# Five edits to a fused two-layer FFN kernel: adapter copies, a wait moved, a group on another engine, a last tile in two parts

## The chip, the cores and the metric

The kernel runs on one core of one Trainium2 chip. The metric is the device time of one execution in microseconds (us). Engines are TensorE (PE in the rows), VectorE (DVE), ScalarE (ACT), GpSimd (POOL) and SyncE (SP), which issues most transfers; its queue is SPq. Each engine runs its own instructions in order, and semaphores order the engines among themselves.

## The reference

Two layers act on `x`, 1024 tokens by 512 features. Each is `x = x + ffn(cond(x))`.

```python
# layer 0: gated net with low-rank adapters picked by token block, then a gated FFN with scaled weights
gate = x @ Wg.T + lora(x);  up = x @ Wu.T + lora(x)        # 1376 hidden
c = (silu(gate) * up) @ Wd.T + lora(...)
f = anemll(silu(anemll(c, gate)) * anemll(c, up), down)     # w_eff = w * (su @ sv), 1792 hidden
x = x + f
# layer 1: one adapted linear, then a gated FFN with group-scaled int4 weights
c = x @ W.T + b + 2 * (x @ A[id]) @ B[id]
f = (silu(c @ Wg.T) * (c @ Wu.T)) @ Wd.T                    # W[o, i] = q[o, i] * s[o, i // 128]
x = x + f
```

## The kernel before, in words

Tokens lie along the free axis in two chunks of 512, features along the partitions in tiles of 128. A float32 operand is split into a rounded part (`_hi`) and a rest (`_lo`), and a product is the sum of three (`hi*hi`, `hi*lo`, `lo*hi`), except with int4 weights, which need two. ScalarE writes the `_hi` parts (activation with Copy), VectorE the `_lo` parts (`lo`, L1221). A written-out order per engine and semaphores decide everything: there is no scheduler.

The phases run in order: `cond` gate/up and down, `ffn0` gate/up and down in two halves, `cond1`, and then the int4 FFN in groups.

**`ffn0` gate/up** takes each weight tile's 2x2 blocks in Strassen's way: seven block products per tile instead of eight (`seven_tile`), issued for tile 0 in the order 2, 6, 4, 3, 1, 5, 7 and for later tiles 2, 3, 1, 4, 5, 6, 7. VectorE scales the raw weights (L1238, L1228), forms their block sums (`block_sums`, L1458, L1461, L1463), subtracts the rests (`piece_lo`), and adds up the products (`part_sum`, `diff`, `gate`, `up`). For tile 0 the product 6 is in `ps_down[0]`, and `seven_gate1` (L1495) reads it; product 3 of tile 1 writes this bank. Behind product 1 of tile 1 TensorE makes scales for the next pair of tiles (`pair_scales`, L1797), which waits for two scale products of VectorE.

**`ffn0 down b`** has four output tiles. Between its second and third, and third and fourth, the adapter rows of `cond1` are made (`hi_of_b1`, `lo_of_b1`), two of four pairs each time. The rows stand in `b1_rows` in four quarters of 32 partitions: hi, lo, hi, lo. `down_adapters` reads them in `cond1`.

**The int4 FFN** runs in two halves (`part`), each of 7 gate/up tiles ("units") and then 4 `down` tiles. A group is one 128-column block of int4 weights times 1024 tokens, four matmuls into one of four PSUM banks in turn. Each group must be read out with its scale, by ScalarE (`scaled`, the first and third) or by VectorE with an add (`added`, L1346), before its bank is used again four groups later (`bank_free`). GpSimd adds partial sums (`unit_join` L809), multiplies half of the tokens of silu(gate) and up (`unit_product` L815), makes `act_lo` (`unit_lo` L820) and adds the `down` results into `xp` (`down_sums` L826, L830, L833). VectorE multiplies the other half (`unit_product` L1354). The `down` groups (o, k) go: (0,0..4), (1,0..4), (0,5), (1,5), (0,6), (1,6), (2,0..6), (3,0..6).

The last `down` tile of the second half uses int4 groups for the first 512 tokens (`half_group`), added up by VectorE (L1406 is the last step), and weights scaled beforehand for the other 512 (`last_rest`, 21 matmuls, added by L1410 in two pieces). SP sends the outputs in order, L720 and L722.

Of the kernel before, what the change touches and what calls it, by code (L numbers as in the profile page):

```python
# [138 lines left out]
def plan_groups():  # L139
# [8 lines left out]
    for part in range(2):  # L148
# [14 lines left out]
def adaln_ffn(nc, d, out):  # L163
# [7 lines left out]
    with ExitStack() as ctx:  # L171
# [79 lines left out]
        down_more = [place(f"down_more{n}", [P, TOK], F32, x) for n, x in enumerate((at["lora_b1"], at["lora_b1"] + 4 * KB, at["h"] + 28 * KB))]  # L251
        w_int = place("w_int", [P, 2, WT], I32, at["w"] + 16 * KB)
# [57 lines left out]
        b1_hi_done, b1_step, b1_ready = sem("b1_hi_done"), sem("b1_step"), sem("b1_ready")  # L310
# [26 lines left out]
        rest_ready, last_sum = sem("rest_ready"), sem("last_sum")  # L337
        sum_done = sem("sum_done")
# [91 lines left out]

        def int_slot(n):

            return (named["cond1"].s0 + HK - 2 + n) % 2
# [163 lines left out]
        def _(sp):  # L597
# [54 lines left out]
            for ph in phases:  # L652
# [74 lines left out]
        def _(pool):  # L727
# [120 lines left out]
        def _(act):  # L848
# [50 lines left out]
            def hi_of_b1(pair):  # L899
# [4 lines left out]
                nc.scalar.activation(b1_rows[quarter(0), pair, :], raw, ACT.Copy)  # L904
                nc.scalar.activation(b1_rows[quarter(2), pair, :], raw, ACT.Copy).then_inc(b1_hi_done, 1)
# [46 lines left out]
            def unit_hi(u):  # L952
                for c in range(CH):
                    act.wait_ge(half_done[c], u + 1)
# [6 lines left out]
            def group_tile(n, u, begun):  # L961
# [3 lines left out]
                if u > 2:  # L965
                    for c in range(CH):
                        act.wait_ge(half_done[c], u - 2)
# [10 lines left out]
            def group_down(n, part, o):  # L978
# [7 lines left out]
                if o == 0:  # L986
                    unit_silu(last)
                if n + 2 < 2 * (ACT_TILES + HK):
# [222 lines left out]
        def _(dve):  # L1211
# [137 lines left out]
            def unit_product(u):  # L1349
# [3 lines left out]
                gate = gate_sum[:, u % 4, chunk(0)]  # L1353
# [815 lines left out]
```

## Time and profile before

| | |
|---|---|
| median of 3 runs | 640.85 us (640.57 to 641.29) |
| the profiled execution: time, span | 641.1 us, 639.5 us |
| TensorE busy | 627.1 us, 98% of the span |
| VectorE, ScalarE, GpSimd busy | 464.0, 322.0, 245.0 us |
| a matmul of 128x512 | about 0.39 us shown, one issued every 0.23 us |

Busy times overlap. In a timeline row a start and a duration stand first, and in brackets how long the engine was idle before it and who released it. A duration can hold a wait inside the instruction. A merged row (x2, x4) covers several instructions.

### The profile page before, as it was taken

Reading aid. Unit: us, or ns where it says so; the run is one execution under the profiler, and the core shown is the slowest. Engines: PE = TensorE matmul, PEld = TensorE weight load, DVE = VectorE, ACT = ScalarE, POOL = GpSimd, SP = SyncE. Lnnn points to the kernel's source line nnn. Section 1 sums busy time; section 2 is a strip of 40 time slices with the busy share of each in tenths; the row PEclk is TensorE's granted clock in tenths of the full one; section 3 lists DMA queues with packets and bytes.
Section 4 is the critical chain, followed back from the end, with each engine's and each line's share of the span. In section 5 each row is a group of like instructions: output and inputs, shape, how many; then the busy total and the mean of one; then the engine's idle time right before and its main releaser. Section 6 shows DMA issues by size and latency. Waiting matters only on the chain.

```text
span 639.5 us, 7875 instructions
## 1 busy us (share of the span) xinstructions
PE 627.1 (98%) x2843; PEld 514.0 (80%) x2843; DVE 464.0 (73%) x569; ACT 322.0 (50%) x430; POOL 245.0 (38%) x192
## 2 busy tenths in 40 slices
PE   8999999999999989999999999999999999999997
PEld 6888888888878878788888778887887887788875
DVE  5576674534467997885447888647688999999997
ACT  5674725244535344442113453435557886578850
POOL 3550020000000025752023666430003888959986
PEclk9999999999999999999999999999999999999999
DMA  8750132101021112311102011240223111221203
GB/s 251 167 149 20 33 92 79 66 1 45 19 73 43 57 34 68 130 58 58 39 27 99 33 34 45 71 86 16 69 92 99 61 58 63 99 67 61 87 0 133
DMA packets 24186, 44.51 MB, mean 70 GB/s; under 512 B 9828, under 2 KB 11876, under 8 KB 24100
## 3 DMA queue, kind: packets, MB, share of 16 engines
q1 hardware_dynamic: 22100, 40.80, 20.8%
q0 software_dynamic: 2048, 3.22, 1.9%
q8 instruction: 23, 0.38, 0.2%
q14 instruction: 15, 0.12, 0.1%
HBM read 40.59 MB, written 2.10 MB: 67 GB/s over the span
## 4 chain that ended last, share of the span: by engine, by line
PE 79%; DVE 8%; ACT 5%; issue 4%; POOL 2%; DMA 1%; SPq 0%; DVEq 0%; ACTq 0%
PE ps_down L1747 7%; PE ps_down L1749 7%; PE ps_down L1748 7%; PE ps_up L1747 3%; PE ps_up L1748 3%; PE ps_up L1749 3%; PE ps_m L1918 3%; PE ps_gate L1918 3%; PE ps_gate L1919 3%; PE ps_down L1919 3%; PE ps_m L1919 3%; PE ps_down L1918 3%; PE ps_up L1918 3%; PE ps_up L1919 3%; PE ps_gate L1747 2%
## 5 line engine op out<-in xcount | busy, mean ns | idle before, releaser
L782 POOL TENSOR_TENSOR act_lo<-up,act_hi 128x512 fp32r<-128x512 f32 x14 | 18.2, 1300 | 194.6 <-ACT act_hi L1033 194.6
L1747 PE MATMUL ps_down<-act_hi,w_hi 128*128 128x512 f32 (+1 forms) x180 | 70.7, 393 | 1.0 <-DVE xp L1568 1.0
L1749 PE MATMUL ps_down<-act_hi,w_lo 128*128 128x512 f32 (+1 forms) x180 | 70.2, 390 | 0.0
L1748 PE MATMUL ps_down<-act_lo,w_hi 128*128 128x512 f32 (+1 forms) x180 | 70.2, 390 | 0.0
L809 POOL TENSOR_TENSOR up_sum<-up_sum,up_more 128x1024 f32<-128x1024 f32 x14 | 33.8, 2413 | 67.0 <-DVE up_more L1346 67.0
L1221 DVE TENSOR_TENSOR w_lo<-w_raw,w_hi 128x512 fp32r<-128x512 f32 (+4 forms) x41 | 44.7, 1090 | 16.0 <-ACT w_hi L866 10.4
L866 ACT ACTIVATE w_hi<-w_raw 128x1024 fp32r<-128x1024 f32 (+4 forms) x30 | 27.0, 900 | 46.0 <-DVE w_raw L1228 23.1
L1221 DVE TENSOR_TENSOR b_rows<-b_raw,b_hi 32x1024 fp32r<-32x1024 f32 (+2 forms) x27 | 28.1, 1042 | 19.9 <-ACT b_rows L884 12.0
L1747 PEld LDWEIGHTS ps_down<-act_hi,w_hi 128*128 128x128 f32 (+1 forms) x180 | 33.8, 188 | 8.1 <-DVE w_lo L1221 1.4
L1749 PEld LDWEIGHTS ps_down<-act_hi,w_lo 128*128 128x128 f32 (+1 forms) x180 | 33.8, 188 | 7.2
L1748 PEld LDWEIGHTS ps_down<-act_lo,w_hi 128*128 128x128 f32 (+1 forms) x180 | 33.8, 188 | 6.8
L820 POOL TENSOR_TENSOR act_lo<-gate_sum,act_hi 128x1024 fp32r<-128x1024 f32 x14 | 39.2, 2806 | 0.0
L944 ACT ACTIVATE act_hi<-gated 128x512 fp32r<-128x512 f32 (+1 forms) x22 | 13.8, 632 | 49.8 <-DVE gated L1330 49.8
L1346 DVE SCALAR_TENSOR_TENSOR gate_sum<-ps_up,s_group,gate_sum 128x1024 f32<-128x1024 f32 x28 | 35.8, 1279 | 3.9 <-PE ps_up L1919 3.9
L1747 PE MATMUL ps_up<-h_hi,w_hi 128*128 128x512 f32 (+1 forms) x96 | 37.7, 393 | 0.3 <-DVE w_lo L1221 0.3
L1748 PE MATMUL ps_up<-h_lo,w_hi 128*128 128x512 f32 (+1 forms) x96 | 37.6, 392 | 0.0
L1749 PE MATMUL ps_up<-h_hi,w_lo 128*128 128x512 f32 (+1 forms) x96 | 37.4, 390 | 0.0
L1027 ACT ACTIVATE w_hi<-w_total 128x512 fp32r<-128x512 f32 (+1 forms) x28 | 20.7, 739 | 32.6 <-POOL w_total L776 21.5
L1568 DVE TENSOR_TENSOR xp<-xp,ps_down 128x512 f32<-128x512 f32 x20 | 13.5, 683 | 28.7 <-PE ps_down L1749 27.3
L1221 DVE TENSOR_TENSOR w_lo<-w_total,w_hi 128x512 fp32r<-128x512 f32 (+1 forms) x28 | 25.4, 909 | 10.8 <-ACT w_hi L1027 10.5
L1747 PE MATMUL ps_gate<-h_hi,w_hi 128*128 128x512 f32 (+1 forms) x80 | 31.6, 395 | 0.5 <-DVE h_lo L1221 0.3
L1861 PE MATMUL ps_gate<-x_hi,w_hi 128*128 128x512 f32 x80 | 31.5, 394 | 0.0
(292 smaller groups left out, 1858.4 us busy)
## 6 DMA issues: line engine op xcount, KB each, us to landing
w_int<-in_ffn_gu SPq DMA_DIRECT2D x14, 512.0 KB, 3.5
w_raw<-in_cond_gu SPq DMA_DIRECT2D x9, 512.0 KB, 4.3
w_raw<-in_ffn_gu SPq DMA_DIRECT2D x9, 512.0 KB, 3.5
w_raw<-in_ffn_dn SPq DMA_DIRECT2D x8, 448.0 KB, 3.2
w_int<-in_ffn_dn SPq DMA_DIRECT2D x8, 448.0 KB, 3.2
xp<-in_x SPq DMA_DIRECT2D x8, 256.0 KB, 5.1
w_raw_third<-in_ffn_gu SPq DMA_DIRECT2D x4, 512.0 KB, 3.4
xp<-in_x SPq DMA_DIRECT2D x1, 2048.0 KB, 10.7
```

The lines of the kernel that those rows point to most:

```text
L809: nc.gpsimd.tensor_tensor(up_sum[:, u % 3, :], up_sum[:, u % 3, :], up_more[:, u % 2, :], ALU.add).then_inc(up_done, 1)
L820: nc.gpsimd.tensor_tensor(act_lo[:, j, :], gate_sum[:, u % 4, :], act_hi[:, j, :].bitcast(F32), ALU.subtract).then_inc(unit_ready, 1)
L866: nc.scalar.activation(w_hi[:, s, n], w_raw[:, s, n], ACT.Copy).then_inc(w_hi_done, 1)
L1027: nc.scalar.activation(w7_hi[j % 2][:, pieces[piece]], value, ACT.Copy).then_inc(done, 1)
L1221: return nc.vector.tensor_tensor(out_, value, hi.bitcast(F32), ALU.subtract)
L1346: return nc.vector.scalar_tensor_tensor(out=here, in0=group_bank(g), scalar=group_scale(g), in1=here, op0=ALU.mult, op1=ALU.add)
L1747: nc.tensor.matmul(ps[0:m, :], w_hi[0:r, s, cols], rhs_hi(k, r), start=start and n == 0, stop=False)
L1748: nc.tensor.matmul(ps[0:m, :], w_hi[0:r, s, cols], rhs_lo(k, r), start=False, stop=False)
L1749: last = nc.tensor.matmul(ps[0:m, :], w_lo[0:r, s, cols], rhs_hi(k, r), start=False, stop=stop and n == len(ks) - 1)
L1861: nc.tensor.matmul(banks[n][:, :], w7_hi[s][:, cols], x_hi[n][:, k, :], start=not more and k == 0, stop=False, skip_group_check=more)
L1918: nc.tensor.matmul(bank[:, chunk(c)], weights, hi[:, chunk(c)], start=True, stop=False)
L1919: last = nc.tensor.matmul(bank[:, chunk(c)], weights, lo[:, chunk(c)], start=False, stop=True)
```

## The change

1. **Adapter rows of `cond1`.** ScalarE and VectorE write only the first hi and lo quarters; SP copies these 64 partitions to the other 64, two pairs at a time, behind the first and second weight loads of `cond1`.
2. **Tile 1 of the Strassen phase** waits for `gate1_done` at its product 3, no longer at its start. On VectorE, `seven_gate1` of tile 0 stands ahead of two block sums.
3. **Group (1,4)** of each half goes from VectorE to ScalarE, into a buffer `down_extra` of its own, and GpSimd adds it (`extra_sum`). VectorE multiplies all 1024 tokens of a half's last unit, and GpSimd none of them.
4. **`last_rest`** runs as two parts of 256 tokens with 21 matmuls each, in two banks, each followed by its add.

```diff
-                    add(n + o, "d", k, "a" if k in (0, 2) else "v")
+                    add(n + o, "d", k, "a" if k in (0, 2) or (o, k) == (1, 4) else "v")
...
+        down_extra = place("down_extra", [P, TOK], F32, at["gated"])
...
+        def halves_done(u, c):
+            return u + 1 - c * ((u + 1) // ACT_TILES)
...
+        rest_quarters = [(last_bank(n)[:, 0:CT // 2], slice(CT + part * CT // 2, CT + (part + 1) * CT // 2))
+                         for part, n in enumerate((ACT_TILES, 0))]
...
                         load_tile(ph, o // 2, o % 2)
+                        if ph.name == "cond1" and o < 2:
+                            sp.wait_ge(b1_ready, 2 * o + 2)
+                            pairs_of = slice(2 * o, 2 * o + 2)
+                            sp.dma_start(b1_rows[2 * PR:4 * PR, pairs_of, :].bitcast(F32),
+                                         b1_rows[0:2 * PR, pairs_of, :].bitcast(F32)).then_inc(b1_copied[o], 16)
...
+            def extra_sum(part):
+                here = xp[:, 1, :]
+                pool.wait_ge(act_read, group_of[part * (ACT_TILES + HK) + ACT_TILES + 1, "d", 4].ea)
+                nc.gpsimd.tensor_tensor(here, here, down_extra[:, :], ALU.add).then_inc(extra_added, 1)
...
                     unit_join(u)
-                    unit_product(u)
+                    if j + 1 < ACT_TILES:
+                        unit_product(u)
                     if j > 0:
                         unit_lo(u - 1)
                 unit_lo(ACT_TILES * (part + 1) - 1)
+                extra_sum(part)
...
                 nc.scalar.activation(b1_hi[quarter(3), pair, :], raw, ACT.Copy)
-                nc.scalar.activation(b1_rows[quarter(0), pair, :], raw, ACT.Copy)
-                nc.scalar.activation(b1_rows[quarter(2), pair, :], raw, ACT.Copy).then_inc(b1_hi_done, 1)
+                nc.scalar.activation(b1_rows[quarter(0), pair, :], raw, ACT.Copy).then_inc(b1_hi_done, 1)
...
+                if o == 1:
+                    if part:
+                        act.wait_ge(extra_added, part)
+                    scaled(group_of[n, "d", 4], down_extra[:, :])
...
-                lo(b1_rows[quarter(1), pair, :], raw, hi).then_inc(b1_step, 1)
-                dve.wait_ge(b1_step, pair + 1)
-                lo(b1_rows[quarter(3), pair, :], raw, hi).then_inc(b1_ready, 1)
+                lo(b1_rows[quarter(1), pair, :], raw, hi).then_inc(b1_ready, 1)
...
-                gate = gate_sum[:, u % 4, chunk(0)]
-                nc.vector.tensor_tensor(gate, gate, up_sum[:, u % 3, chunk(0)], ALU.mult).then_inc(half_done[0], 1)
+                tokens = chunk(0) if (u + 1) % ACT_TILES else slice(0, TOK)
+                gate = gate_sum[:, u % 4, tokens]
+                nc.vector.tensor_tensor(gate, gate, up_sum[:, u % 3, tokens], ALU.mult).then_inc(half_done[0], 1)
...
+                if (q, n) == (1, 3):
+                    pe.wait_ge(gate1_done, 1)
...
-                if q == 1:
-                    pe.wait_ge(gate1_done, 1)
...
                 pe.wait_ge(last_ready, 2)
+                for n, (bank, tokens) in enumerate(rest_quarters):
+                    if n == 1:
+                        pe.wait_ge(act_read, groups[-ACT_TILES].ea)
```

What stands where on an engine, first VectorE in the Strassen phase, at the end of tile 0. `part_sum`, `gate` and `up` are tile 0's partial results, `w_total` the block sums and `w_lo` the rests of tile 1's weights, and `ps_*` the banks. Before:

```order
L1221 TENSOR_TENSOR w_lo_91<-w_total_95,w_hi_89 128x512 [waits piece_hi_done]
L1461 TENSOR_TENSOR w_total_95<-w_raw 128x256
L1463 TENSOR_TENSOR w_total_95<-w_raw 128x512
L1495 TENSOR_TENSOR gate_0_106<-ps_down,part_sum_100 128x512 [waits part_done,seven_done]
L1538 TENSOR_TENSOR part_sum_100<-part_sum_100,ps_gate 128x512 [waits seven_done,part_done]
L1221 TENSOR_TENSOR w_lo_91<-w_total_95,w_hi_89 128x768 [waits w_hi_done]
L1550 TENSOR_TENSOR up_0_102<-ps_gate,part_sum_100 128x512 [waits seven_done,rest_done]
```

After the change:

```order
L1250 TENSOR_TENSOR w_lo_91<-w_total_95,w_hi_89 128x512 [waits piece_hi_done]
L1524 TENSOR_TENSOR gate_0_106<-ps_down,part_sum_100 128x512 [waits part_done,seven_done]
L1490 TENSOR_TENSOR w_total_95<-w_raw 128x256
L1492 TENSOR_TENSOR w_total_95<-w_raw 128x512
L1567 TENSOR_TENSOR part_sum_100<-part_sum_100,ps_gate 128x512 [waits seven_done,part_done]
L1250 TENSOR_TENSOR w_lo_91<-w_total_95,w_hi_89 128x768 [waits w_hi_done]
L1579 TENSOR_TENSOR up_0_102<-ps_gate,part_sum_100 128x512 [waits seven_done,rest_done]
```

The `gate` sum (L1495 before, L1524 now) moved ahead of both block sums.

GpSimd at the end of the second half, from the last unit on, `act_lo` being the rests and `xp` the output. Before:

```order
L809 TENSOR_TENSOR up_sum<-up_sum,up_more 128x1024 [waits dve_read]
L815 TENSOR_TENSOR gate_sum<-gate_sum,up_sum 128x512 [waits up_done,gate_done]
L820 TENSOR_TENSOR act_lo<-gate_sum,act_hi 128x1024 [waits unit_hi_done] x2
L826 TENSOR_TENSOR xp<-xp,down_more_123 128x1024 [waits dve_read]
L830 TENSOR_TENSOR xp<-xp,down_sum 128x1024 [waits dve_read,more_added]
L826 TENSOR_TENSOR xp<-xp,down_more_124 128x1024 [waits dve_read]
L830 TENSOR_TENSOR xp<-xp,down_sum 128x1024 [waits dve_read,more_added]
L826 TENSOR_TENSOR xp<-xp,down_more_122 128x1024 [waits dve_read]
L833 TENSOR_TENSOR xp<-xp,down_sum 128x512 [waits dve_read,more_added]
```

After the change:

```order
L826 TENSOR_TENSOR up_sum<-up_sum,up_more 128x1024 [waits dve_read]
L837 TENSOR_TENSOR act_lo<-gate_sum,act_hi 128x1024 [waits unit_hi_done] x2
L842 TENSOR_TENSOR xp<-xp,down_extra 128x1024 [waits act_read]
L850 TENSOR_TENSOR xp<-xp,down_more_123 128x1024 [waits dve_read]
L854 TENSOR_TENSOR xp<-xp,down_sum 128x1024 [waits dve_read,more_added]
L850 TENSOR_TENSOR xp<-xp,down_more_124 128x1024 [waits dve_read,extra_added]
L854 TENSOR_TENSOR xp<-xp,down_sum 128x1024 [waits dve_read,more_added]
L850 TENSOR_TENSOR xp<-xp,down_more_122 128x1024 [waits dve_read]
L857 TENSOR_TENSOR xp<-xp,down_sum 128x512 [waits dve_read,more_added]
```

The 512-column product is gone, so the two `act_lo` follow the join at once, and an add of `down_extra` stands ahead of all other adds.

VectorE at the start of the `down` groups of the second half, from group (0,1) on. Before:

```order
L1346 SCALAR_TENSOR_TENSOR down_sum<-ps_m,s_down,down_sum 128x1024 [waits group_ready,act_read]
L1346 SCALAR_TENSOR_TENSOR down_more_123<-ps_up,s_down,down_more_123 128x1024 [waits group_ready,act_read]
L1354 TENSOR_TENSOR gate_sum<-gate_sum,up_sum 128x512 [waits up_done,gate_done]
L1346 SCALAR_TENSOR_TENSOR down_sum<-ps_gate,s_down,down_sum 128x1024 [waits group_ready,dve_read]
L1346 SCALAR_TENSOR_TENSOR down_sum<-ps_down,s_down,down_sum 128x1024 [waits group_ready,act_read]
L1346 SCALAR_TENSOR_TENSOR down_more_124<-ps_gate,s_down,down_more_124 128x1024 [waits group_ready,act_read]
L1346 SCALAR_TENSOR_TENSOR down_sum<-ps_m,s_down,down_sum 128x1024 [waits group_ready,dve_read]
L1346 SCALAR_TENSOR_TENSOR down_more_123<-ps_down,s_down,down_more_123 128x1024 [waits group_ready,dve_read]
L1346 SCALAR_TENSOR_TENSOR down_more_124<-ps_up,s_down,down_more_124 128x1024 [waits group_ready,dve_read]
```

After the change:

```order
L1373 SCALAR_TENSOR_TENSOR down_sum<-ps_m,s_down,down_sum 128x1024 [waits group_ready,act_read]
L1373 SCALAR_TENSOR_TENSOR down_more_123<-ps_up,s_down,down_more_123 128x1024 [waits group_ready,act_read]
L1382 TENSOR_TENSOR gate_sum<-gate_sum,up_sum 128x1024 [waits up_done,gate_done]
L1373 SCALAR_TENSOR_TENSOR down_sum<-ps_gate,s_down,down_sum 128x1024 [waits group_ready,dve_read]
L1373 SCALAR_TENSOR_TENSOR down_sum<-ps_down,s_down,down_sum 128x1024 [waits group_ready,act_read]
L1373 SCALAR_TENSOR_TENSOR down_more_124<-ps_gate,s_down,down_more_124 128x1024 [waits group_ready,act_read]
L1373 SCALAR_TENSOR_TENSOR down_more_123<-ps_down,s_down,down_more_123 128x1024 [waits group_ready,dve_read]
L1373 SCALAR_TENSOR_TENSOR down_more_124<-ps_up,s_down,down_more_124 128x1024 [waits group_ready,dve_read]
```

The product (`gate_sum<-gate_sum,up_sum`) has 1024 columns, and one read of bank `ps_m`, that of group (1,4), is gone.

## Rows read from the trace of the kernel before

**Rows 1.** Stretches of 20 us: busy time per engine, granted clock, DMA share, GB/s

```profile
...
220.00:240.00 20.00, 18.23 (x83) 14.80 (x82) 19.43 (x32) 9.79 (x17) 4.75 (x4) 1.00 0.17 53
...
620.00:640.00 20.00, 14.94 (x64) 11.51 (x63) 15.33 (x17) 3.30 (x4) 14.03 (x7) 0.94 0.29 106
...
```

**Rows 2.** Waits of TensorE: waiting, waited for, us, times, longest

```profile
...
PE ps_gate L1918 <- DVE down_sum L1346: 1.5, 2, 0.7
...
```

**Rows 3.** Timeline, Strassen tiles 0 and 1 (start, us, idle before and its releaser)

```profile
228.92 0.68 DVE L1221 TENSOR_TENSOR w_lo<-w_total,w_hi 128x512 fp32r<-128x512 f32 x1
...
231.65 0.95 DVE L1221 TENSOR_TENSOR w_lo<-w_total,w_hi 128x768 fp32r<-128x768 f32 x1
...
235.11 0.68 DVE L1238 TENSOR_TENSOR w_raw_third<-w_raw_third,ps_m 128x512 f32<-128x512 f32 x1
...
230.57 0.84 ACT L1027 ACTIVATE w_hi<-w_total 128x768 fp32r<-128x768 f32 x1 [2.11 <-DVE w_total L1463]
...
231.24 0.47 PE L1861 MATMUL ps_up<-x_hi,w_hi 128*128 128x512 f32 x1 [1.49 <-DVE gate L1495]
...
235.85 0.74 PE L1797 MATMUL ps_m<-pack_long,pack_short 128*128 128x256 f32 x4 [0.28 <-DVE w_raw_third L1238]
```

**Rows 4.** Timeline, second and third tile of `ffn0 down b`

```profile
430.29 0.63 ACT L903 ACTIVATE b_hi<-b_raw 32x512 fp32r<-32x512 f32 x1
...
433.51 0.63 ACT L905 ACTIVATE b_rows<-b_raw 32x512 fp32r<-32x512 f32 x1
...
434.17 1.41 DVE L1221 TENSOR_TENSOR b_rows<-b_raw,b_hi 32x512 fp32r<-32x512 f32 x2 [0.53 <-ACT b_rows L905]
435.61 1.09 DVE L1228 TENSOR_TENSOR w_raw<-w_raw,ps_m 128x896 f32<-128x896 f32 x1
...
438.79 1.28 DVE L1568 TENSOR_TENSOR xp<-xp,ps_down 128x512 f32<-128x512 f32 x2
...
438.22 0.39 PE L1749 MATMUL ps_down<-act_hi,w_lo 128*128 128x512 f32 x1
439.61 0.47 PE L1747 MATMUL ps_down<-act_hi,w_hi 128*128 128x512 f32 x1 [1.00 <-DVE xp L1568]
```

**Rows 5.** Timeline, end of the first half; last row groups by line

```profile
530.59 2.42 POOL L809 TENSOR_TENSOR up_sum<-up_sum,up_more 128x1024 f32<-128x1024 f32 x1
533.68 1.30 POOL L815 TENSOR_TENSOR gate_sum<-gate_sum,up_sum 128x512 f32<-128x512 f32 x1 [0.68 <-ACT gate_sum L950]
534.93 2.86 POOL L820 TENSOR_TENSOR act_lo<-gate_sum,act_hi 128x1024 fp32r<-128x1024 f32 x1
...
533.90 1.64 DVE L1354 TENSOR_TENSOR gate_sum<-gate_sum,up_sum 128x512 f32<-128x512 f32 x1
535.46 1.27 DVE L1346 SCALAR_TENSOR_TENSOR down_sum<-ps_gate,s_down,down_sum 128x1024 f32<-128x1024 f32 x1
...
536.78 0.50 PE L1918 MATMUL ps_gate<-act_hi,w_q 128*128 128x512 f32 x1 [0.74 <-DVE down_sum L1346]
...
545.40 0.50 PE L1918 MATMUL ps_m<-act_hi,w_q 128*128 128x512 f32 x1
...
L1354 DVE TENSOR_TENSOR gate_sum<-gate_sum,up_sum 128x512 f32<-128x512 f32 x14 | 11.7, 832 | 0.0
```

**Rows 6.** Timeline, the end of the program

```profile
619.52 2.41 POOL L826 TENSOR_TENSOR xp<-xp,down_more 128x1024 f32<-128x1024 f32 x1 [1.69 <-DVE down_more L1346]
...
631.71 2.55 POOL L833 TENSOR_TENSOR xp<-xp,down_sum 128x512 f32<-128x512 f32 x2
...
621.23 1.12 ACT L959 ACTIVATE down_sum<-ps_down,s_down 128x1024 f32<-128x1024 f32 x1 [0.86 <-PE ps_down L1919]
...
633.35 1.47 DVE L1406 TENSOR_TENSOR xp<-xp,down_sum 128x512 f32<-128x512 f32 x1
...
634.29 0.33 SPq L720 DMA_DIRECT2D out_t<-xp  x1
...
635.81 0.45 SPq L722 DMA_DIRECT2D out_t<-xp  x1
```

More of the change, by code:

```diff
@@ L309, in adaln_ffn @@
         a1_hi_done, a1_ready = sem("a1_hi_done"), sem("a1_ready")
-        b1_hi_done, b1_step, b1_ready = sem("b1_hi_done"), sem("b1_step"), sem("b1_ready")
+        b1_hi_done, b1_ready = sem("b1_hi_done"), sem("b1_ready")
+        b1_copied = [sem(f"b1_copied{n}") for n in range(2)]
         pack_hi_done, pack_step, pack_ready = sem("pack_hi_done"), sem("pack_step"), sem("pack_ready")
@@ L337, in adaln_ffn @@
         rest_ready, last_sum = sem("rest_ready"), sem("last_sum")
+        extra_added = sem("extra_added")
         sum_done = sem("sum_done")
@@ L824, in down_sums @@
                 here = xp[:, o, :]
+                if o == 1:
+                    pool.wait_ge(extra_added, part + 1)
                 pool.wait_ge(dve_read, group_of[n, "d", 5].ev)
@@ L966, in group_tile @@
                     for c in range(CH):
[L967 removed]
+                        act.wait_ge(half_done[c], halves_done(u - 3, c))
                 scaled(group_of[n, "u", 0], up_sum[:, u % 3, :])
@@ L1381, in group_down @@
                     unit_product(ACT_TILES * (part + 1) - 1)
-                dve.wait_ge(dve_read, group_of[n, "d", 1].ev)
-                added(group_of[n, "d", 4], both).then_inc(dve_read, 1)
+                if o != 1:
+                    dve.wait_ge(dve_read, group_of[n, "d", 1].ev)
+                    added(group_of[n, "d", 4], both).then_inc(dve_read, 1)
             def group_down_more(n, part, o):
@@ L1390, in group_down_end @@
             def group_down_end(n, part, o):
-                dve.wait_ge(dve_read, group_of[n, "d", 4].ev)
+                dve.wait_ge(dve_read, group_of[n, "d", 1 if o == 1 else 4].ev)
                 added(group_of[n, "d", 6], down_sum[:, (HK * part + o) % 3, :]).then_inc(dve_read, 1)
             def last_tile(n, m):
-                both, (here, rest) = down_sum[:, m % 3, chunk(0)], (xp[:, HK - 1, chunk(c)] for c in range(CH))
+                both, here = down_sum[:, m % 3, chunk(0)], xp[:, HK - 1, chunk(0)]
                 dve.wait_ge(act_read, group_of[n, "l", 0].ea)
@@ L1406, in last_tile @@
                 nc.vector.tensor_tensor(here, here, both, ALU.add).then_inc(last_sum, 1)
-                dve.wait_ge(rest_ready, 1)
-                bank = last_bank(ACT_TILES)
-                for tokens in (slice(0, CT // 2), slice(CT // 2, CT)):
-                    nc.vector.tensor_tensor(rest[:, tokens], rest[:, tokens], bank[:, tokens], ALU.add).then_inc(last_sum, 1)
+                for n, (bank, tokens) in enumerate(rest_quarters):
+                    dve.wait_ge(rest_ready, n + 1)
+                    rest = xp[:, HK - 1, tokens]
+                    nc.vector.tensor_tensor(rest, rest, bank, ALU.add).then_inc(last_sum, 1)
             def last_weights():
@@ L1928, in last_rest @@
             def last_rest():
-                bank = last_bank(ACT_TILES)
                 pe.wait_ge(last_ready, 2)
-                for k in range(ACT_TILES):
-                    part = int(k * P >= last_cut)
-                    cols = slice(k * P - part * last_cut, (k + 1) * P - part * last_cut)
-                    hi, low = (act[:, k, chunk(1)] for act in (act_hi, act_lo))
-                    nc.tensor.matmul(bank, last_hi[part][:, cols], hi, start=k == 0, stop=False)
-                    nc.tensor.matmul(bank, last_hi[part][:, cols], low, start=False, stop=False)
-                    last = nc.tensor.matmul(bank, last_lo[part][:, cols], hi, start=False, stop=k == ACT_TILES - 1)
-                last.then_inc(rest_ready, 1)
+                for n, (bank, tokens) in enumerate(rest_quarters):
+                    if n == 1:
+                        pe.wait_ge(act_read, groups[-ACT_TILES].ea)
+                    for k in range(ACT_TILES):
+                        part = int(k * P >= last_cut)
+                        cols = slice(k * P - part * last_cut, (k + 1) * P - part * last_cut)
+                        hi, low = (act[:, k, tokens] for act in (act_hi, act_lo))
+                        nc.tensor.matmul(bank, last_hi[part][:, cols], hi, start=k == 0, stop=False)
+                        nc.tensor.matmul(bank, last_hi[part][:, cols], low, start=False, stop=False)
+                        last = nc.tensor.matmul(bank, last_lo[part][:, cols], hi, start=False, stop=k == ACT_TILES - 1)
+                    last.then_inc(rest_ready, 1)
             def bank_free(g):
@@ L1981, in down_adapters @@
                 if ph.name == "cond1":
-                    pe.wait_ge(b1_ready, PAIRS)
+                    for n in range(2):
+                        pe.wait_ge(b1_copied[n], 16)
                     pe.wait_ge(t_hi_rows, 2 * CH + c + 1)
```

5 lines of the change are left out of this document (3 added, 2 removed).

## Prediction

> **What bounds the kernel now.** I read the span in stretches of 20 us first. TensorE is busy nearly everywhere (98% of the span) at the higher of its two clock levels; the two stretches with the most time without it are shown: from 220 us 1.8 us, at a granted clock of 1.00 and with VectorE busy 19.4 of 20, and the last with 5.1 [rows 1]. Then TensorE's waits: 1.5 us go to a VectorE read of a `down` group, twice [rows 2]. So time is won only where TensorE pauses, or behind its last product. Then the timelines of the four places that the diff touches [rows 3 to 6]. All sums are made against the profiled execution's own time, 641.1 us (span 639.5 and 1.6 around it), which is 0.25 above the median, 640.85. No change smaller than about 0.2% (1.3 us) can be told from none.
>
> **Strassen tile 1, expected gain 1.5 us, taken as a loss of 0.4.** TensorE waits 1.49 us before product 2 of tile 1, which starts at 231.24, for the gate sum L1495 [rows 3]. Now only product 3 waits for it, and L1495 stands two instructions earlier. Product 2 can start once the piece subtraction at 228.92 is done, near 229.7, so products 2, 3 and 1 go 1.5 us early. But the next thing in TensorE's queue is a pair of scales that waits for VectorE's second scale product, L1238 at 235.11; before, TensorE already waited 0.28 for it, until 235.85 [rows 3]. VectorE runs with no pause over 0.1 us from 228.92 to there and none of its work goes away, so TensorE only waits later. Worse, the two block sums slip by the 0.60 of L1495. ScalarE's 0.84 us rounding of piece 2 needs them: it started at 230.57 and ended at 231.41, before VectorE wanted it at 231.65. Now it starts at 231.17 and VectorE gets it about 0.88 after its start, at 232.05. VectorE's chain, and with it the scales and all behind, goes from 231.65 to 232.05: **+0.40**. Bounds: 0 if the rounding is quicker than that row, and a gain of 1.5 if VectorE had slack that I can't see.
>
> **Next net's adapter rows.** Each of four pairs loses a ScalarE copy of 0.64 us and a VectorE subtraction with its self wait; in their place stand two transfers. The loss matters for pairs 0 and 1 only: TensorE paused from 438.45 (0.23 after its last issue at 438.22) to 439.61 for the sum L1568 at 438.79 [rows 4]. Before, ScalarE ran six activations from 430.29, the last at 433.51, and VectorE's second pair started at 434.17. With four, ScalarE ends pair 1 at about 432.85, VectorE subtracts from 432.89 to 433.5, and L1228 starts at 433.5, not 435.61: 2.1 us earlier. All up to L1568 hangs on it, so that starts at 436.7 and TensorE does not wait: 439.61 - 438.45 = 1.16, and 0.08 for the first product after a pause, which is slower: **-1.24**. The transfers are issued by SP at about 433.6 and 442; the product that reads the rows runs after 460, and a wait of SP for them ends before the wait of the load behind it (the weight buffer comes free at 437 and 446). So they cost nothing; without that cover each would cost the 2.0 to 2.5 us of an SP transfer. Bounds: gain 1.0 to 1.3.
>
> **End of each half: the product that VectorE takes over.** VectorE's product for unit 6 (L1354) doubles from 512 to 1024 columns; a fourth of a `down` tile's seven groups, (1,4), goes to ScalarE; GpSimd loses its half product and gets a 1024-column add. Before, VectorE asked for L1354 at 533.90, while GpSimd held L815 from 533.68 to about 534.93; the product ended at 535.46, which is 0.53 after GpSimd was done, and GpSimd's next instruction (L820) took 2.86 where a 1024-column one takes 2.4 [rows 5]. So these two instructions ran one after the other. After the change GpSimd has no product at 533.68: it goes from L809 (530.59, done 2.37 later at 532.96) straight into L820, 2.36 long, until 535.32. VectorE asks at 533.90, waits until 535.32, and then needs 1.07 for 1024 columns (twice the 0.53): done at 536.39, **0.93 later** than 535.46. Its next read, L1346, is the one that TensorE waits for: group (1,3) starts at 537.71, not 536.78. After that VectorE has one 1.2 us read less, so the small pause before 545.40 and its slow first products go (0.16 and 0.12 there, 0.12 one group earlier): 0.40 comes back. **+0.53** per half; what is queued behind the product on VectorE are the reads that free banks for TensorE, and ScalarE's rounding of unit 6 behind it, with (1,2) and the new (1,4), is late by 0.9 but ahead of TensorE.
> Without the wait (both engines side by side) the product would end at 533.90 + 1.2 = 535.1, 0.36 earlier than before, and a half would gain 0.76. The mean of all L1354, 0.83 us, seems to speak for this. The Trainium skill (SBUF, State Buffer; section "Who interferes with whom") says that a VectorE instruction with two SBUF inputs and a GpSimd instruction that reads SBUF fully block each other, and whichever comes first keeps the port for its whole length; by it the half loses 0.53, by the mean alone it gains. The rows at 533.90 and 534.93 agree with the rule.
>
> **Behind the second half: GpSimd.** From 619.52 GpSimd adds `down` results without a pause until L833 ends, 631.71 + 2.55, near 634.24 [rows 6]. The new add of `down_extra` comes first. It needs ScalarE's read of (1,4): TensorE's group (1,3) at 614.47 + 0.93 = 615.40, (1,4) 1.05 later at 616.45, ScalarE's read starts 1.10 after the group did and takes 1.12 with 0.04 until others see it, as that of the next `down` tile does at 621.23: 618.71. The add takes 2.36, until 621.07, so the chain starts 1.55 late and ends at 635.79. VectorE's add L1406 now meets it too: it asks near 633.9 while the first L833 runs, gets in between the two, and puts 0.53 on the second: 636.32. SP sends outputs in order, so the send that left at 634.29 leaves at 636.37; the other three follow at the 0.38 at which sends follow each other, and the last leaves at 637.51, not 635.81: **+1.70**, the half's own +0.53 in it.
> The last half tile in two parts is hidden under this: 42 products of 256 columns for 21 of 512. Four with 256 columns and their own weights took 0.74 us with the slow first one [rows 3], against 0.23 of pace for 512, so 42 take 4.8 to 5.1 where 21 took 4.76; VectorE's first part is done before the second is ready and saves 0.33. TensorE's side would end at 636.0, before the sends. Uncovered it is worth -0.2 to +0.1.
>
> **Sum:** +0.40 - 1.24 + 0.53 + 1.70 = +1.39: 642.5 for the profiled execution, **642.2** for the median.
>
> **Rivals.**
> 1. TensorE keeps the 1.5 us of tile 1 (scales not bound by VectorE). Against it: the 0.28 wait at 235.85. Then -1.5 in place of +0.40: sum -0.51, 640.3. Chance 0.12.
> 2. GpSimd is not what ends the kernel, because it catches up or the extra add fits its pause before 619.52 (1.7 us long). Against it: (1,4) is read only by 618.7. Then +0.68 (0.53, 0.15 of shorter products) in place of 1.70: +0.37, 641.2. Chance 0.15.
> 3. The other side: the product is not blocked. Then each half gains 0.76, of which the sends at the end keep 0.15: +0.40 - 1.24 - 0.76 - 0.15 = -1.75, 639.1. It decides from the point where L1354 with 1024 columns ends before 535.2. Against it: the rows at 533.90 and L1406's 1.47 for 512 columns beside L833. Chance 0.09, with mixtures 0.12.
> 4. Worse: the last four sends are closer together than before, so the data queue is what ends; then the shift of the first of them, 2.08, counts whole, and VectorE's delay is not given back (+0.93 for +0.53): 640.85 + 0.40 - 1.24 + 0.93 + 2.48 = 643.4. Chance 0.11.
> The forecast, 641.5 to 642.9, has 0.50.
>
> **Numbers.** 80% range 640.3 to 643.3. Faster by over 0.2% (below 639.6) holds rival 3 and a rest: 0.12. Slower (above 642.1) holds rival 4 and three quarters of the forecast: 0.49. Within: 0.39.
>
> **What would show it.** Right: product 2 of tile 1 near 229.7, and the wait at the scales grown to about 2.5 us; no wait before 439.6 (shifted); the 1024-column product taking over 2.4 us, and TensorE's wait behind it grown to about 1.7; GpSimd's last adds ending after TensorE's last product, and SP waiting for them. Wrong: a product of 1.2 us, or a last send that waits for L1410's successor on VectorE.

## The result and the profile after

In five executions the changed kernel took 644.48 us in the median (643.16 to 644.68), the kernel before 641.29 in the same comparison: a ratio of 1.0044, interval 1.0025 to 1.0062. Slower was right; 644.48 is 2.3 above the 642.2 predicted and 1.2 above the top of the range. Of these 2.3, 0.44 is not the change's: the forecast was counted from 640.85, and the kernel before took 641.29 in this comparison. The change cost 3.2, where 1.4 was forecast.

The profiled execution is the fastest of the five, 643.16, with a span of 641.2 at a mean granted TensorE clock of 0.997. The other four spanned 642.4 to 642.7 at 0.995. So this trace can show where 1.7 us went, and not the rest. First its stretches of 20 us (columns as in [rows 1]) and TensorE's waits, against [rows 1, 2].

```profile
220.00:240.00 20.00, 17.82 (x82) 14.44 (x81) 19.10 (x32) 9.69 (x17) 4.40 (x4) 1.00 0.16 53
620.00:640.00 20.00, 15.34 (x88) 13.28 (x86) 15.04 (x17) 3.83 (x4) 15.73 (x8) 0.94 0.29 106
```

```profile
PE ps_gate L1947 <- DVE down_sum L1373: 3.3, 2, 1.7
PE ps_m L1826 <- DVE w_raw_third L1267: 2.2, 1, 2.2
```

The wait for the gate sum is gone, and the wait for the scale product is 2.2 where it was 0.28; the one for the `down` reads has grown from 1.5 to 3.3. Between 220 and 240 TensorE works less than before, not more. The timeline of tile 1, against [rows 3]:

```profile
229.46 0.68 DVE L1524 TENSOR_TENSOR gate<-ps_down,part_sum 128x512 f32<-128x512 f32 x1
...
231.99 0.96 DVE L1250 TENSOR_TENSOR w_lo<-w_total,w_hi 128x768 fp32r<-128x768 f32 x1 [0.32 <-ACT w_hi L1056]
...
235.46 0.68 DVE L1267 TENSOR_TENSOR w_raw_third<-w_raw_third,ps_m 128x512 f32<-128x512 f32 x1
...
231.11 0.85 ACT L1056 ACTIVATE w_hi<-w_total 128x768 fp32r<-128x768 f32 x1 [2.70 <-DVE w_total L1492]
...
229.06 0.63 PE L1826 MATMUL ps_m<-pack_long,pack_short 128*128 128x256 f32 x4
229.69 0.47 PE L1890 MATMUL ps_up<-x_hi,w_hi 128*128 128x512 f32 x1
...
236.19 0.74 PE L1826 MATMUL ps_m<-pack_long,pack_short 128*128 128x256 f32 x4 [2.18 <-DVE w_raw_third L1267]
```

Product 2 starts 1.55 earlier, the scales 0.34 later (0.40 against the first scales of tile 1, which are at 229.06 here and at 229.12 before). VectorE now waits 0.32 for the rounding on ScalarE. At the adapter rows, against [rows 4], VectorE:

```profile
433.23 0.68 DVE L1250 TENSOR_TENSOR b_rows<-b_raw,b_hi 32x512 fp32r<-32x512 f32 x1 [0.61 <-ACT b_rows L930]
433.94 1.09 DVE L1257 TENSOR_TENSOR w_raw<-w_raw,ps_m 128x896 f32<-128x896 f32 x1
...
437.12 0.68 DVE L1597 TENSOR_TENSOR xp<-xp,ps_down 128x512 f32<-128x512 f32 x1
```

The sum that TensorE needs starts 1.67 earlier, and TensorE has no wait there. The end of the first half, against [rows 5]:

```profile
532.00 2.41 POOL L837 TENSOR_TENSOR act_lo<-gate_sum,act_hi 128x1024 fp32r<-128x1024 f32 x1
...
532.95 2.55 DVE L1382 TENSOR_TENSOR gate_sum<-gate_sum,up_sum 128x1024 f32<-128x1024 f32 x1
535.42 1.27 DVE L1373 SCALAR_TENSOR_TENSOR down_sum<-ps_gate,s_down,down_sum 128x1024 f32<-128x1024 f32 x1
...
536.75 0.50 PE L1947 MATMUL ps_gate<-act_hi,w_q 128*128 128x512 f32 x1 [1.66 <-DVE down_sum L1373]
```

GpSimd's instruction ends at 534.41; the product is asked for at 532.95 and ends at 535.50, 1.09 behind it. And the end of the program, against [rows 6]:

```profile
618.42 2.40 POOL L842 TENSOR_TENSOR xp<-xp,down_extra 128x1024 f32<-128x1024 f32 x1 [1.08 <-ACT down_extra L984]
620.78 2.41 POOL L850 TENSOR_TENSOR xp<-xp,down_more 128x1024 f32<-128x1024 f32 x1
...
632.98 2.99 POOL L857 TENSOR_TENSOR xp<-xp,down_sum 128x512 f32<-128x512 f32 x2
...
617.22 1.12 ACT L984 ACTIVATE down_extra<-ps_m,s_down 128x1024 f32<-128x1024 f32 x1 [1.36 <-PE ps_m L1948]
...
635.38 0.42 DVE L1439 TENSOR_TENSOR xp<-xp,ps_m 128x256 f32<-128x256 f32 x1 [0.22 <-PE ps_m L1969]
...
637.35 0.44 SPq L739 DMA_DIRECT2D out_t<-xp  x1
```

GpSimd works without a pause from the extra add to its end at 635.97, behind VectorE's last add; the last send leaves 1.54 later than before.

### The profile page after: what moved, and what is told of

Its sections match the earlier page's. It is cut to its first block, busy times and chain, and to the rows that moved or that the text cites. A ratio compares the mean times of both kernels' runs of the same rounds, so it can differ in the third digit from the quotient of the medians.

```text
span 641.2 us, 7918 instructions
## 1 busy us (share of the span) xinstructions
PE 625.7 (98%) x2864; PEld 515.7 (80%) x2864; DVE 461.4 (72%) x563; ACT 321.7 (50%) x428; POOL 247.0 (39%) x192
## 3 DMA queue, kind: packets, MB, share of 16 engines
q0 software_dynamic: 2048, 3.22, 2.0%
## 4 chain that ended last, share of the span: by engine, by line
PE 77%; DVE 7%; ACT 5%; issue 5%; POOL 4%; DMA 1%; POOLq 0%; SPq 0%; DVEq 0%; ACTq 0%
PE ps_down L1776 7%; PE ps_down L1777 7%; PE ps_down L1778 7%; PE ps_up L1776 3%; PE ps_up L1777 3%; PE ps_up L1778 3%; PE ps_m L1947 3%; PE ps_gate L1947 2%; PE ps_m L1948 2%; PE ps_down L1948 2%; PE ps_gate L1948 2%; PE ps_down L1947 2%; PE ps_gate L1776 2%; PE ps_gate L1777 2%; PE ps_gate L1778 2%
## 5 line engine op out<-in xcount | busy, mean ns | idle before, releaser
L1250 DVE TENSOR_TENSOR b_rows<-b_raw,b_hi 32x1024 fp32r<-32x1024 f32 (+2 forms) x23 | 25.4, 1104 | 18.6 <-ACT b_rows L910 12.0
```

The source lines that it names most:

```text
L1250: return nc.vector.tensor_tensor(out_, value, hi.bitcast(F32), ALU.subtract)
```

## The experiments

Twelve kernels ran, in three groups of four: from the changed kernel again to the one without the Strassen part, from the adapter rows to the wait moved, and from the half tile on. Each group ran on a chip of its own, together with 24 to 35 executions of the kernel before (medians 641.07, 641.07 and 641.02). The table gives each one's median with the number of executions, its ratio with the interval, and a column read from its trace: the span less the start of the first scales of tile 1 (229.12 in the trace before, so 410.38 there). Nothing that an edit touches lies ahead of that row, yet it starts between 228.55 and 230.94 in these traces; taking it off makes single traces comparable. Spans are read to 0.1, so this column is good to about 0.1. The row in the trace before:

```profile
229.12 0.63 PE L1797 MATMUL ps_m<-pack_long,pack_short 128*128 128x256 f32 x4
```

The table's last column is what the time holds beside the span, in the mean.

| kernel | median (n) | ratio | span from tile 1, against before | beside the span |
|---|---|---|---|---|
| before | 641.07 (35) | | 0 | 1.62 |
| changed, first comparison | 644.48 (5) | 1.0044, 1.0025 to 1.0062 | +1.76 | 1.97 |
| changed again | 643.21 (7) | 1.0040, 1.0024 to 1.0056 | +3.22 | 1.99 |
| Strassen part only | 642.25 (11) | 1.0011, 1.0001 to 1.0020 | +0.40 | 1.62 |
| half end only | 643.74 (5) | 1.0041, 1.0028 to 1.0054 | +2.67 | 1.86 |
| changed without Strassen part | 642.65 (12) | 1.0032, 1.0018 to 1.0046 | +1.25 | 1.99 |
| adapter rows only | 639.85 (12) | 0.9981, 0.9967 to 0.9996 | -1.28 | 1.81 |
| group moved only | 642.51 (12) | 1.0022, 0.9998 to 1.0046 | +0.78 | 1.79 |
| whole product only | 642.75 (12) | 1.0025, 1.0012 to 1.0038 | +1.78 | 1.63 |
| wait moved only | 640.77 (12) | 0.9998, 0.9984 to 1.0011 | -0.01 | 1.61 |
| half tile in two only | 640.98 (12) | 1.0002, 0.9993 to 1.0011 | 0.00 | 1.65 |
| Strassen part, pause filled | 641.36 (12) | 1.0006, 0.9998 to 1.0015 | +0.40 | 1.61 |
| changed, pause filled | 643.05 (10) | 1.0030, 1.0018 to 1.0042 | +1.75 | 1.99 |
| rows and first half's group | 639.84 (12) | 0.9977, 0.9967 to 0.9987 | -1.66 | 1.69 |

**Changed kernel again.** No edit.

> The changed kernel once more, unchanged. Its profiled execution spanned 641.2 us at a mean granted TensorE clock of 0.997, and four others 642.4 to 642.7 at 0.995. Theory T1 (the clock): in most executions the clock falls to its lower level for a stretch of TensorE's work, which costs some 1.3 us (0.002 of 641 us); expected is a median 2.9 to 3.3 us above the kernel before, executions in two groups (spans near 641.2 at 0.997 and near 642.5 at 0.995), and, if the profile falls on one of the second group, a stretch ahead of TensorE's last product with a granted clock under 1.00. Theory T2 (no clock: transfers, or the drift between runs): spans spread evenly, and their clocks don't go with them.

Two groups came: spans of 640.5 to 641.2 at 0.997 to 0.998 (four), and 643.2, 643.7 and 644.5 at 0.995 (three). This time the profiled execution is of the second group. Its windows of 1 us behind the pause at tile 1 (columns as in [rows 1], the third number from the end is the granted clock as a share of 2.4 GHz):

```profile
235.00:236.00 1.00, 0.90 (x4) 0.40 (x3) 0.90 (x2) 0.00 (x0) 0.00 (x0) 1.00 0.38 53
236.00:237.00 1.00, 0.00 (x0) 0.00 (x0) 1.00 (x3) 0.77 (x2) 0.00 (x0) 1.00 0.78 283
...
238.00:239.00 1.00, 0.95 (x6) 0.86 (x7) 0.96 (x2) 0.00 (x0) 1.00 (x2) 0.86 0.00 0
239.00:240.00 1.00, 1.00 (x4) 0.81 (x3) 1.00 (x3) 0.06 (x1) 0.54 (x2) 0.50 0.00 0
240.00:241.00 1.00, 1.00 (x4) 0.81 (x3) 0.90 (x2) 0.58 (x1) 1.00 (x1) 0.50 0.06 16
241.00:242.00 1.00, 1.00 (x4) 0.73 (x3) 0.82 (x1) 0.67 (x2) 1.00 (x2) 0.50 0.00 0
242.00:243.00 1.00, 1.00 (x6) 0.83 (x5) 0.00 (x0) 0.44 (x1) 1.00 (x2) 0.93 0.00 0
```

And TensorE's timeline there:

```profile
238.04 0.74 PE L1826 MATMUL ps_m<-pack_long,pack_short 128*128 128x256 f32 x4 [2.15 <-DVE w_raw_third L1267]
238.62 0.53 PE L1890 MATMUL ps_up<-x_hi,w_hi 128*128 128x512 f32 x1
238.95 0.63 PE L1891 MATMUL ps_up<-x_lo,w_hi 128*128 128x512 f32 x1
239.38 0.63 PE L1892 MATMUL ps_up<-x_hi,w_lo 128*128 128x512 f32 x1
239.80 0.63 PE L1890 MATMUL ps_up<-x_hi,w_hi 128*128 128x512 f32 x1
...
241.94 0.49 PE L1892 MATMUL ps_down<-x_hi,w_lo 128*128 128x512 f32 x1
242.27 0.39 PE L1890 MATMUL ps_down<-x_hi,w_hi 128*128 128x512 f32 x1
```

The shares 0.86, three times 0.50 and 0.93 mean that the clock went to the lower of its two levels, 1.2 GHz, at about 238.7 and came back at about 242.1: some 0.7 us after TensorE came back from its pause, and for about 3.4 us. Products of 512 columns follow each other at 0.43 us, where the same products at 2.4 GHz keep 0.23. By the second scales behind these (at 260.22, against 256.91 in the first trace) this had cost 1.47: counted from the first scales of tile 1, that row comes after 29.32 instead of 27.85. That is the whole difference between the two traces of this kernel in the table, 3.22 and 1.76. The theory of the clock (T1) stands. The rest of this execution's 646.52 is 1.84 us lost at the start of the program, ahead of every edit.

**Strassen part only.** `seven_gate1` ahead of the block sums, and TensorE's wait at product 3:

```diff
                 if q == 0:
+                    seven_gate1(ph, j)
                     for part in (1, 2):
                         block_sums(ph, 1, part)
-                    seven_gate1(ph, j)
...
+                if (q, n) == (1, 3):
+                    pe.wait_ge(gate1_done, 1)
...
-                if q == 1:
-                    pe.wait_ge(gate1_done, 1)
```

> Only the Strassen part of the change, everything else as before. By the trace of the changed kernel VectorE's chain and all behind it go +0.34 to +0.40 us. T1a (the clock falls behind the longer pause at tile 1, 2.2 us idle where it was 0.3 after an earlier one of 1.5): +1.6 to +1.7 us in most executions, spans near 641.2 at 0.995. T1b (the clock falls behind one of the other pauses, the 1.66 us before group (1,3) or the end) and T2: +0.4 us, spans near 639.9, clock 0.997. The prediction's rival that TensorE keeps the 1.5 us: -1.5.

Five of eleven executions have a clock of 0.996 or 0.997 and spans of 640.6 to 641.5; five have 0.999 and 639.3 to 639.8. The eleventh is the profiled one, with 0.999: it kept the clock through a pause of 2.15, and its 641.0 has 1.1 from the start. Its pause, and the clock where the trace of the changed kernel had 0.50:

```profile
237.36 0.73 PE L1797 MATMUL ps_m<-pack_long,pack_short 128*128 128x256 f32 x4 [2.15 <-DVE w_raw_third L1238]
```

```profile
239.00:240.00 1.00, 1.00 (x6) 0.80 (x5) 0.90 (x3) 0.73 (x2) 0.69 (x1) 1.00 0.07 16
240.00:241.00 1.00, 1.00 (x6) 0.82 (x5) 1.00 (x1) 0.75 (x2) 1.00 (x2) 1.00 0.00 0
```

So the trace gives +0.40 and the executions that lost the clock about 1.3 more: theory T1a, with a chance of about one half, not "most".

**Half end only.** The edits of the whole change to the groups, the extra add and the product (the diffs stand at the two experiments that do one of them each), nothing else.

> Only the end of each half changed (group (1,4) to ScalarE, the extra add on GpSimd, unit 6's product whole on VectorE). By the trace of the changed kernel: +0.57 for the first half, +1.92 behind the second and 0.16 more behind the last send, +2.6 us together. T1a: +2.6, clock as before. T1b: +3.9 in most executions, with a clock 0.002 lower. Rival 3 of the prediction (product not blocked): -0.5 or better.

+2.67 in the trace and 643.74 in the median: its pauses of 1.66 and 1.67 at 537 and 615 don't cost clock (0.999 in three of five, 0.997 at worst). T1b is out.

**Changed without Strassen part.** The whole change less the diff of the Strassen part.

> The changed kernel without its Strassen part. By the trace: -1.24 + 0.57 + 1.92 + 0.16 = +1.4 us. T1a: the median is +1.4 us (1.7 to 1.8 us faster than the changed kernel), all spans near 640.9, clock 0.997. T1b or T2: only 0.35 faster than the changed kernel, +2.8 us.

+1.25, and eleven of twelve executions span 640.2 to 641.5 at 0.998 or 0.999. The twelfth, 645.5 at 0.996, has its like in the kernel before (643.8 and 644.5 at 0.997, two of 35). The second group is gone with the Strassen part: T1a. The median says less. It is 1.6 above the kernel before, near the +1.4 of T1a and far from the +2.8 of T1b; but it is only 0.56 under that of the changed kernel next to it, of which four executions in seven had kept their clock, and 1.8 under that of the first comparison.

**Adapter rows only.**

```diff
+                        if ph.name == "cond1" and o < 2:
+                            sp.wait_ge(b1_ready, 2 * o + 2)
...
+                            sp.dma_start(b1_rows[2 * PR:4 * PR, pairs_of, :].bitcast(F32),
+                                         b1_rows[0:2 * PR, pairs_of, :].bitcast(F32)).then_inc(b1_copied[o], 16)
...
-                nc.scalar.activation(b1_rows[quarter(2), pair, :], raw, ACT.Copy).then_inc(b1_hi_done, 1)
...
-                lo(b1_rows[quarter(3), pair, :], raw, hi).then_inc(b1_ready, 1)
```

> Only the next net's adapter rows by transfers. The theory of the prediction, which the trace of the changed kernel bears out: -1.24 us, 639.8 us, no wait of TensorE near 438, and no clock effect (spans near 638.2). Rival: the transfers collide with weight loads or SP's queue elsewhere and give part back: -0.9 to 0.

-1.28 in the trace and 639.85 in the median, where 639.8 was expected. The gain is whole: inside the span nothing of it is given back. Only the time beside the span is longer, by 0.2.

**Group moved only.** With the waits that go with it; the product is split as before.

```diff
-                    add(n + o, "d", k, "a" if k in (0, 2) else "v")
+                    add(n + o, "d", k, "a" if k in (0, 2) or (o, k) == (1, 4) else "v")
...
+                nc.gpsimd.tensor_tensor(here, here, down_extra[:, :], ALU.add).then_inc(extra_added, 1)
...
+                    scaled(group_of[n, "d", 4], down_extra[:, :])
```

> Only the group (1,4) moved to ScalarE with its extra add on GpSimd; unit 6's product stays split between VectorE and GpSimd. Theory G (two causes): TensorE's wait before group (1,3) stays at 0.7 to 0.8, the first half gains 0.4, and behind the second half GpSimd's chain starts some 1.0 to 1.4 late, since TensorE is not late: +0.6 to +1.0 us together, 641.7 to 642.1. Rival H (the extra add with its wait for ScalarE is nearly all of it): +2.2 to +2.6, 643.5. A gain of 0.4 or more would mean that GpSimd isn't what ends the kernel.

+0.78 in the trace, inside theory G's range. The median, 642.51, is not: it lies 0.4 above that range, and its interval reaches from no change to nearly +3 us, so it excludes neither theory. Of the twelve spans five are near 639.8 like the trace's, six lie between 640.4 and 642.4 with clocks of 0.997 to 0.999, and one is 646.6 at 0.992; no run tells why, and the readings here are the trace's. TensorE's wait before group (1,3) is 0.74 as before. The second half's (1,3) starts 385.00 us after the first scales of tile 1 instead of 385.35, so the first half gains 0.35; behind the second GpSimd's extra add fills its pause and more:

```profile
617.05 2.41 POOL L827 TENSOR_TENSOR xp<-xp,down_extra 128x1024 f32<-128x1024 f32 x1
619.42 2.41 POOL L835 TENSOR_TENSOR xp<-xp,down_more 128x1024 f32<-128x1024 f32 x1
```

**Whole product only.**

```diff
-                    unit_product(u)
+                    if j + 1 < ACT_TILES:
+                        unit_product(u)
...
-                gate = gate_sum[:, u % 4, chunk(0)]
-                nc.vector.tensor_tensor(gate, gate, up_sum[:, u % 3, chunk(0)], ALU.mult).then_inc(half_done[0], 1)
+                tokens = chunk(0) if (u + 1) % ACT_TILES else slice(0, TOK)
+                gate = gate_sum[:, u % 4, tokens]
+                nc.vector.tensor_tensor(gate, gate, up_sum[:, u % 3, tokens], ALU.mult).then_inc(half_done[0], 1)
```

> Only unit 6's product whole on VectorE (1024 columns), the seven groups shared out as before. Theory G: the product waits for GpSimd's instruction and takes over 2.4 us, TensorE's wait before group (1,3) grows to 1.7 in each half, none of it is given back: +1.5 to +1.9 us, 642.8. Rival H: the product costs little here, +0 to +0.5. Rival 3 of the prediction (no blocking): -0.5 or better, the product 1.2 us.

+1.78 in the trace, that is 0.89 for each half, and 642.75 in the median, where theory G had 642.8. GpSimd and VectorE at the end of the first half:

```profile
534.77 2.43 POOL L825 TENSOR_TENSOR act_lo<-gate_sum,act_hi 128x1024 fp32r<-128x1024 f32 x1
...
535.72 2.56 DVE L1361 TENSOR_TENSOR gate_sum<-gate_sum,up_sum 128x1024 f32<-128x1024 f32 x1
...
539.53 0.50 PE L1925 MATMUL ps_gate<-act_hi,w_q 128*128 128x512 f32 x1 [1.67 <-DVE down_sum L1352]
```

GpSimd ends at 537.20, the product at 538.28. By the traces theory G holds and H falls: the product alone costs 1.78 and the group alone 0.78, 2.56 together where both edits in one kernel cost 2.67.

**Wait moved only.** The last two pieces of the Strassen diff without the first.

> Only TensorE's wait for the gate sum moved from product 2 to product 3 of tile 1; VectorE's order as before, so that nothing on VectorE slips. By the timeline TensorE's pauses of 1.49 and 0.28 become one of about 1.8 before the scales, which start at the same time. Theory T1a with the length of the pause deciding (1.5 keeps the clock, 2.15 loses it): between them, so 0 (641.1) where the clock holds and +1.6 in the executions where it falls, fewer of them than with the pause of 2.15. Rival (the loss is VectorE's order, not the pause): 0 in all executions, clock 0.999. Rival 1 of the prediction: a gain of 1.5.

```profile
235.46 0.74 PE L1797 MATMUL ps_m<-pack_long,pack_short 128*128 128x256 f32 x4 [1.64 <-DVE w_raw_third L1238]
```

-0.01: one pause of 1.64 for two of 1.49 and 0.28, and the scales no earlier. No execution of the twelve is in a second group: the two longest spans, 640.7 and 640.8, have clocks of 1.000 and 0.999. So the pause of 1.64 kept the clock twelve times out of twelve, where those of 2.15 to 2.18 kept it 11 times out of 23. By itself this can't settle the cause, since it is also what the rival forecast (0 in all executions): pause and VectorE's order changed together. The kernels with the filled pause, below, have the order without the pause. The +0.40 is all VectorE's order: without it the scales don't slip.

**Half tile in two only.**

```diff
-                for k in range(ACT_TILES):
+                for n, (bank, tokens) in enumerate(rest_quarters):
...
+                    for k in range(ACT_TILES):
```

> Only the last half tile in two parts, all else as before. Prediction's step: hidden, -0.2 to +0.1 us where nothing covers it, 641.0. TensorE's last 42 products of 256 columns take 4.8 to 5.1 us where 21 of 512 took 4.76; VectorE's and SP's end move by less than 0.3. Rival: 42 products cost 0.5 us or more with nothing given back, 641.6.

0.00 in the trace and 640.98 in the median, as expected. The 42 products take 5.0 us (4.8 to 5.1 expected) where the 21 took 4.8, and VectorE's last add is shorter by 0.33 (0.42 for 0.75). The last send is 0.11 earlier against group (1,3), and the span doesn't have it.

**Pause filled**, in the Strassen part alone and in the whole change. The results of the first pass are overwritten by the second:

```diff
+                    twice = 2 if (q, n) == (1, 1) else 1
-                    for k in range(HK // 2):
+                    for k in [k for _ in range(twice) for k in range(HK // 2)]:
```

> The Strassen part alone, and in it product 1 of tile 1 is computed twice into the same bank (6 more products of 512 columns, the first results overwritten), so that TensorE's pause before the scales is 0.8 us and not 2.15; the scales start when they did. Theory T1a: the clock no longer falls, no execution at 0.996 to 0.997, spans 639.3 to 639.9 as in the undisturbed executions of the Strassen part alone, median 641.2 and not 642.25. Rival (the slow executions of the Strassen part have another cause, such as VectorE's order or the loads): still half of the executions 1.2 us longer at 0.996.

> The whole change with the same filled pause. T1a: one group, spans 640.5 to 641.2 at 0.997 to 0.998, median 642.7, where the changed kernel had 643.2 and 644.5. T1b (clock lost at another pause too) or T2: medians and the 0.995 executions stay as in the changed kernel.

The profiled executions of the two, one row each:

```profile
236.85 0.74 PE L1797 MATMUL ps_m<-pack_long,pack_short 128*128 128x256 f32 x4 [0.80 <-DVE w_raw_third L1238]
```

```profile
235.70 0.74 PE L1826 MATMUL ps_m<-pack_long,pack_short 128*128 128x256 f32 x4 [0.82 <-DVE w_raw_third L1267]
```

The six more products cost nothing: from tile 1 the spans are +0.40 and +1.75, as without them. In the changed kernel the second group is gone: nine of ten executions span 640.6 to 641.3 at 0.998 or 0.999, and the tenth, 643.8 at 0.997, is of the kind that the kernel before has too. In the Strassen part the spans are 639.3 to 640.5 at 0.998 or more, but for one of 641.4 at 1.000; no execution is at 0.996 or 0.997. That shows the cause by putting it right: VectorE's order and the same late scales, a short pause before them, and in 22 executions at most one loss of clock, against 12 in 23 with the long pause. One thing is open: the kernels with the long pause ran in other comparisons and, in the second comparison at least, on another chip than those with the filled one, and were not run beside them. The kernel before doesn't differ between these chips (medians within 0.05), and the loss came in two comparisons. The expected medians are 0.2 and 0.35 under the measured ones, and lie within the intervals.

**Rows and first half's group.** The adapter rows, the half tile in two, and the group with its extra add in the first half:

```diff
-                    add(n + o, "d", k, "a" if k in (0, 2) else "v")
+                    add(n + o, "d", k, "a" if k in (0, 2) or (part, o, k) == (0, 1, 4) else "v")
```

> The parts that gained, put together: adapter rows by transfers, the last half tile in two parts, and the group (1,4) on ScalarE with its extra add in the first half only; unit 6's product split, Strassen part as before. Theory: -1.24 for the rows, -0.35 to -0.4 for the first half's group, 0 to -0.2 for the half tile: -1.6 to -1.8 us, 639.3; clock 0.999. Rival: the gain of the group is given back before the end, since VectorE's chain or the sends end the kernel: -1.2, 639.8.

-1.66 from tile 1, in the range expected, and 639.84, ratio 0.9977 (0.9967 to 0.9987). The trace and the median disagree here. By the trace the kernel beats the adapter rows alone by 0.38; by the medians (639.84 and 639.85) it doesn't, and 639.8 is the rival's number. In the trace nothing is given back before the end, against what the rival said, but the medians of twelve executions that span 637.2 to 640.0 can't show 0.38. Faster than the kernel before is shown, by 0.1% to 0.3%; that the group adds to the adapter rows rests on the traces alone.

## Why the prediction was off

**Strassen tile 1: right as far as it went, and here lies the step that failed.** The chain over VectorE's block sums and ScalarE's rounding gave +0.40, and the scales came 0.40 late in all five traces that have VectorE's new order; "TensorE only waits later" was true. The longer wait was foreseen too, at about 2.5 where 2.15 to 2.18 was measured. But its price was put at nothing, without a reason. Two pauses of 1.49 and 0.28 with products 2, 3 and 1 between them had become one of 2.2, and behind it TensorE lost its clock in 7 of 12 executions of the changed kernel and 5 of 11 of the Strassen part alone, at 1.2 to 1.5 us each time. The sum had no term for this, and no rival held it. In the first comparison four of five executions paid it, so the median did; in the second three of seven, and the median, 643.21, is that of an execution that kept its clock (the first comparison's took 643.16) and inside the predicted range. Which of the two medians comes is chance. The Trainium skill (TensorE: Matmul & The Clock Gate, section "The HAM clock gate") says that the gate watches in a rhythm of its own that doesn't start with the kernel, and that the number of slow products at a kernel's start therefore differs from run to run. The page says this of the start; carried over to a pause, it would be paid in some executions only, and the counts, 12 of 23, agree.

**Adapter rows: right.** -1.24 forecast, -1.28 measured alone. TensorE's pause is gone, and the transfers are hidden.

**End of each half: right, size and mechanism.** The product ends 1.09 behind GpSimd's instruction (1.07 forecast), TensorE's wait is 1.66, and a half costs 0.57 where 0.53 was forecast: the shift against before is -0.95 just ahead of the first half's group (1,3), -0.03 at it, and -0.38 just ahead of the second half's, so 0.92 is paid and 0.35 given back. The two edits alone give 0.89 for each half and -0.35 for the first, together 0.54. Rival 3, the product not blocked, is out: no 1024-column product took under 2.5.

**Behind the second half: right in its steps, and two terms 0.4 too small.** Moved by the same 0.38 that the trace is ahead there, the extra add starts at 618.80 (618.71 forecast), GpSimd ends at 636.35 (636.32), and the first of the last sends leaves at 636.38 (636.37). The last one leaves at 637.73, not 637.51, since three sends took 1.35 instead of three times 0.38; and 0.16 more passed between it and the end of the span. Both were terms taken over from before.

**Half tile in two: right**, 0.00.

**Beside the span: a second term that was missing.** The sum took the 1.6 us between span and time as constant. It is 1.97 in the changed kernel. Alone, the adapter rows have 1.81, the group moved 1.79 and the half end 1.86; the Strassen part, the whole product and the half tile have 1.62 to 1.65. So it comes with the first two of these edits, but the kernel that has both, in the first half, has 1.69. What in them does it, no run here tells; it was not tried further.

So the 3.2 us of the first comparison are: 1.76 from tile 1 on (1.39 forecast, the difference being the 0.22 and 0.16 of the sends), 0.35 beside the span, and some 1.3 of clock in four executions of five. That is 3.4, and the 0.2 left over is less than what the start scatters. Less the 1.4 forecast, and with the 0.44 by which the kernel before was slower in that comparison, the 3.2 are the 2.3 between forecast and median.

## What to carry to other kernels

Before you move a wait, look at what stands behind it in the queue: if that waits for the same busy engine, the wait isn't removed but gathered with the next, and a gathered pause can cost TensorE its clock, as here, where two short ones with work between them didn't. A profile of one execution may be of the kind that kept the clock, so read the mean clock and the span of every execution; where a pause can't be shortened, work whose result is thrown away can fill it, here at no cost. And give a fast engine's work to another only where the other's own end doesn't end the kernel: the same group moved gains 0.35 in the first half and costs 1.1 behind the second, by the traces.

## What was not expected of the hardware

- A pause of TensorE of 1.49, 1.64 or 1.67 kept the granted clock; one of 2.15 to 2.18 lost it in 12 of 23 executions. The fall comes late: in the one trace that has it TensorE had been working again for 0.7 us, and it stayed at 1.2 GHz for 3.4 us, at a price of 1.47.
- VectorE's product of 1024 columns, 2.55 to 2.56 long beside GpSimd's instruction, did not lengthen that one, which took 2.41 to 2.43, where with the product of 512 columns GpSimd's next took 2.86 [rows 5].
- The time beside the span, 1.57 to 1.69 for the kernel before, was 1.94 to 2.02 in all twelve executions of the changed one.
